# Products that nobody reads, added on TensorE at three places of a vision-tower kernel

## The reference

```python
h = tok(x)                                  # patches @ W_lin.T + b, class token, positions
h = h + attn(layernorm(h))                  # 16 query heads of 16, one shared key/value head
h = h + ffn0(layernorm(h))                  # two factored products, gated by entmax15 of 16 logits
h = h + delta(layernorm(h))                 # causal delta rule: solve (I - A0) A = I, read out
h = h + moe(layernorm(h))                   # 8 experts, arg-max router, 256 -> 1024 -> 256, gelu
```

```python
z = z / 2 - max(z / 2);  zs = sort descending(z)
mean, meansq = cumsum(zs) / k, cumsum(zs * zs) / k
tau = mean - sqrt(clip((1 - k * (meansq - mean**2)) / k, 0))
a = square(clip(z - tau[support - 1], 0))       # support = number of tau <= zs
```

## Time and profile before

| | us |
|---|---|
| median of 3 runs | 780.35 (780.12 to 784.51) |
| profiled execution, its own time | 781.44 |
| its span, first to last instruction | 779.7 |
| PE busy | 672.8 (86% of the span) |
| DVE busy | 419.7 (54%) |
| ACT / POOL busy | 246.8 / 292.6 |
| mean granted TensorE clock | 0.925 of full |

### The profile page before, as it was taken

One profiled execution on the slowest core, in us unless ns is written; L12 is line 12 of the kernel. 1 busy time (PEld: TensorE's weight loads), 2 busy tenths in 40 slices (PEclk: granted clock), 3 DMA queues, 4 the chain that ended last, 5 costly groups with the idle time before them and its releaser, 6 DMA issues.

```text
span 779.7 us, 13703 instructions
## 1 busy us (share of the span) xinstructions
PE 672.8 (86%) x4576; PEld 512.7 (66%) x4576; DVE 419.7 (54%) x1120; ACT 246.8 (32%) x679; POOL 292.6 (38%) x483
## 2 busy tenths in 40 slices
PE   5899999999997614999999589495999999999994
PEld 3566776676765413899999567373667676676763
DVE  2456677777665475244389999557233333333331
ACT  0123333333333114344444256261032323222231
POOL 2344544544444100165566777360222222223220
PEclk9899999999998755899999999896799999999998
DMA  8311001111100000000011216698101111211110
GB/s 302 123 36 32 24 21 34 37 36 37 37 2 1 1 0 2 1 6 8 22 24 32 43 45 236 254 362 309 54 28 55 44 59 41 62 41 51 53 34 14
DMA packets 25070, 50.73 MB, mean 65 GB/s; under 512 B 15611, under 2 KB 15741, under 8 KB 24363
## 3 DMA queue, kind: packets, MB, share of 16 engines
q1 hardware_dynamic: 21387, 35.36, 14.1%
q0 software_dynamic: 3328, 10.23, 4.3%
q10 hardware_dynamic: 288, 4.27, 1.3%
HBM read 39.99 MB, written 9.86 MB: 64 GB/s over the span
## 4 chain that ended last, share of the span: by engine, by line
PE 45%; DVE 7%; issue 4%; POOL 3%; ACT 0%; POOLq 0%; DVEq 0%; ACTq 0%
PE psum L1192 12%; PE psum L1168 11%; PE psum L1389 5%; PE psum L1401 4%; PE psum L1181 3%; PE psum L1435 2%; DVE work L1741 1%; PE psum L1369 1%; PE psum L1011 1%; DVE arena_w L1748 1%; PE psum L1379 1%; POOL work L1900 1%; PE psum L1411 1%; PE psum L1441 1%; POOL work L1889 1%
## 5 line engine op out<-in xcount | busy, mean ns | idle before, releaser
L1265 ACT ACTIVATE work<-psum,cst 128x128 f32<-128x128 f32 x208 | 56.6, 383 | 144.1 <-PE psum L1181 144.1
L1168 PE MATMUL psum<-arena_w,work 128*128 x208 | 93.7, 593 | 1.3 <-DVE work L1219 1.3
L1192 PE MATMUL psum<-arena_w,work 128*128 x416 | 94.2, 379 | 0.4 <-ACT work L1265 0.4
L1130 POOL DMA_INDIRECT out<-work,row_i x26 | 25.8, 990 | 158.0 <-DVE work L1241 158.0
L1192 PEld LDWEIGHTS psum<-arena_w,work 128*128 128x128 f32 x416 | 77.1, 190 | 10.5 <-issue 1.1
L1228 DVE COPY work<-psum 128x512 f32<-128x512 f32 x52 | 36.0, 692 | 67.7 <-PE psum L1168 57.4
L347 PE MATMUL psum<-arena_w 128*111 128x256 f32 x264 | 64.3, 397 | 4.9 <-DMA arena_w<-in_pack 4.9
L712 POOL TENSOR_TENSOR arena_w<-arena_w,work 101x592 f32<-101x592 f32 x33 | 39.6, 1200 | 71.8 <-DVE work L578 71.8
L1168 PEld LDWEIGHTS psum<-arena_w,work 128*128 128x128 f32 x208 | 37.5, 190 | 38.8 <-issue 38.8
L347 PEld LDWEIGHTS psum<-arena_w 128*111 128x111 f32 x264 | 46.8, 183 | 19.6 <-issue 9.6
L703 POOL TENSOR_TENSOR arena_w<-arena_w 128x296 f32<-128x296 f32 x66 | 44.0, 690 | 20.7 <-DVE arena_w L546 20.7
(11 more groups left out here) (220 smaller groups left out, 1332.4 us busy)
## 6 DMA issues: line engine op xcount, KB each, us to landing
arena_w<-in_w SPq DMA_DIRECT2D x2, 4096.0 KB, 13.6
arena_w<-in_x SPq DMA_DIRECT2D x22, 333.0 KB, 3.0
x_rows<-tokens SPq DMA_DIRECT2D x22, 192.0 KB, 5.2
arena_w<-in_pack ACTq DMA_DIRECT2D x1, 2442.0 KB, 9.2
cst<-in_packc ACTq DMA_DIRECT2D x1, 1727.0 KB, 13.4
arena_w<-in_pack SPq DMA_DIRECT2D x1, 818.5 KB, 7.0
arena_w<-in_pack SPq DMA_DIRECT2D x2, 384.0 KB, 4.3
arena_w<-n_rows SPq DMA_DIRECT2D x8, 85.6 KB, 2.8
```

What stands on the lines that cost most here:

```text
L1130: pool.indirect_dma_start(out_h, bass.IndirectOffsetOnAxis(ap=row_i[:, 2 * i + j:2 * i + j + 1], axis=0), yo[j], None).then_inc(y_stored[j ...
L1168: mm = nc.tensor.matmul(bank[2 * j + f][:, :], xgt[j][:, k * 128:(k + 1) * 128], arena_w1[:, bass.ds(expert * (2 * FF) + (k * FF + f * 512 ...
L1192: mm = nc.tensor.matmul(bank[7][:, 0:D], ht[j][:, g * 128:(g + 1) * 128], arena_w2[:, bass.ds(expert * (FC * D) + g * D, D)], start=(g == ...
L1265: nc.scalar.activation(ht[j][:, g * 128:(g + 1) * 128], bank[4 + f][:, k * 128:(k + 1) * 128], ACT.Gelu, bias=cst[:, bass.ds(expert * FC + ...
```

## The change

Filling products come in at three places, and nothing is taken out or moved otherwise.

- Stage 2: 23 fillers on PE ahead of the wait for `gates_ready`, into banks 6 and 7 in turn.
- Stage 3: a new helper `fill_start` issues 3 fillers in the turn i = 0, behind `first_products(0)` and ahead of `hidden(0)`.
- Routing: 6 fillers instead of 4 between the counting products and the wait for `lanes_ready`; `keep_busy` takes the banks 3 to 7 in turn, for its index would otherwise leave PSUM. The 3 fillers behind the placing stay.

```diff
             @block.tensor
             def _(pe):
+                for k in range(23):
+                    nc.tensor.matmul(bank[6 + k % 2], ident, cst[:, 0:512], start=True, stop=True)
                 pe.wait_ge(gates_ready, 1)
...
             def keep_busy(pe, times):
 
                 for k in range(times):
-                    nc.tensor.matmul(bank[3 + k], ident, cst[:, 0:512], start=True, stop=True)
+                    nc.tensor.matmul(bank[3 + k % 5], ident, cst[:, 0:512], start=True, stop=True)
+
+            def fill_start(pe, times):
+
+                for k in range(times):
+                    nc.tensor.matmul(bank[6 + k % 2], ident, cst[:, 0:512], start=True, stop=True)
...
-                keep_busy(pe, 4)
+                keep_busy(pe, 6)
                 for t in range(NT):
                     pe.wait_ge(lanes_ready, t // 4 + 1)
...
                 for i in range(-1, PAIRS + 2):
                     second_products(i - 1)
                     first_products(i)
+                    if i == 0:
+                        fill_start(pe, 3)
```

## The result

| | before | after |
|---|---|---|
| median of the runs of one session | 781.82 us (6 runs, 780.12 to 786.28) | 775.30 us (6 runs, 774.55 to 776.52) |
| ratio, 95% interval | | 0.9911 (0.9881 to 0.994) |
| the same once more, in a later session (e8 below) | 780.36 us | 775.14 us, ratio 0.9945 (0.9922 to 0.9967) |
| span of the profiled execution | 779.7 us | 773.1 us |

The change makes the kernel 4 to 7 us faster. 777.4 was predicted, with 773.0 to 781.5 as the range.

The account below looks back on a forecast made before the run. PE was taken to bound the kernel, running at half clock after waits at the start of stage 3 and in the routing. 0 - 1.8 + 2.1 - 3.6 - 0.7 = -4.0 us from 781.44 gave 777.4 us, range 773.0 to 781.5.

Parts of the forecast that it names:

- The 23 fillers: Stage 2, ahead of the gates' transposes: hidden by DVE's work with 0.2 to 1.5 us to spare, cost 0.
- c: Stage 2: delay until the clock rises under the fillers, taken as 3.4 to 6.0 us; they end at 297.4 + c/2.
- Transposes and copies: End of stage 2: the 22 transposes start at full clock and the last copy ends sooner, gain 1.8 us.
- Three fillers: Stage 3, behind `first_products(0)`: cost 2.1 us on the path at full clock, 4.6 us at half clock.
- The cold stretch: Start of stage 3, PE at half clock for 9.3 us: gain 3.6 us, between bounds of 2.5 or so and 4.7.
- the fear of the pause: Barrier between stages 2 and 3, about 302.7 to 304.4: the clock may be lost, leaving 2.5 or so of 4.7 us.
- The routing: Two more fillers let placing start at full clock: gain 1.2 us, 0.5 charged back behind, net 0.7 us.
- Stages behind move as a whole: Behind feed-forward: later engines' chains start from its end, so those stages shift unchanged.
- Rival A: Between stages 2 and 3: clock lost in the pause, three fillers at half clock; gain about 2, 779.4 us; chance 0.20.
- Rival B: Stage 3 and routing: clock holds through the pause and all placing products; -8.7, 772.7 us; chance 0.08.
- Rival C: Stage 2: fillers get the clock late or never and overrun the gates; slower, up to 793.8 us; chance 0.06.
- rival D: Start of stage 3: the 10.17 us cold stretch is only the profiled execution's; 780.0 us; chance 0.20.

Follow-up runs that it names:

- e8: The whole change run once more, in a later session, against the kernel before; 775.14 us, ratio 0.9945.
- e6: The whole change with 32 instead of 23 fillers ahead of the gates; one execution, 784.31 us.
- e1: The kernel before plus only the 23 fillers ahead of the gates' transposes; 774.93 us, ratio 0.9937.
- e4: The whole change without the three fillers of `fill_start`; 774.79 us, ratio 0.9934.
- e10: The whole change with 2 instead of 3 fillers behind the placing; 778.40 us, ratio 0.9965.
- e3: The kernel before with only the routing's fillers raised from 4 to 6; 780.12 us, ratio 1.0003.
- e11: The kernel before, unchanged, profiled a second time; one execution, 778.45 us.
- e2: The kernel before plus only the three fillers behind `first_products(0)`; 779.29 us, ratio 0.9989.
- e5: The whole change with 15 instead of 23 fillers ahead of the gates; one execution, 778.85 us.
- e7: The whole change with one filler added in the pause, one instead of three behind `first_products(0)`, four in the routing; 777.36 us, ratio 0.9969.

## Why the prediction was right

- The 23 fillers. 297.4 + c/2 with c = 5.3 and a start 1.2 us sooner gives 298.9; they ended at 299.2, with 0.19 us to spare where 0.2 to 1.5 were forecast. No cost, and e6 shows what it is when the cover is gone.
- Transposes and copies: -1.8 forecast, -1.80 measured, in the profile and again in e1 and e4 (26.64 and 26.65).
- Three fillers: +2.1 forecast, +1.78 measured. The 0.3 lies within the overlap of neighbouring PE records.
- The cold stretch: -3.6 forecast, -4.62 measured against the profile of before, which is its upper bound of 4.7: the clock held. Taking a value between the two bounds was a hedge, and neither the profile of the changed kernel nor e8 or e10 lies between them. e1, e4 and e6 show that the fear of the pause was right: there the clock is lost for 3.4 us, in e6 under the three fillers themselves. With them or without them the sum is the same within 0.15 us.
- The routing: -0.7 forecast, -1.69 in the profiles. Neither number is shown to be the change's: e3's ratio is 1.0003, and e11 has the short placing without the two fillers. This term of the sum has no support in the runs.
- "Stages behind move as a whole" held within 0.3 us against e11, where the delta rule's second half took 88.30 us at a mean clock of 0.87, as in the changed kernel (88.33, 0.87). The +0.95 us against the first profile (0.89) are that execution's. In other versions the stretch took up to 91.1 us at 0.82, and the forecast allowed nothing for that.
- The time. 777.4 was added up from an execution of 781.44 us, 1.1 us above the median of its runs. Between the two profiled executions the times differ by 6.6 us, where the sum has 4.0. Of the 2.6 us missing, 1.0 is the cold stretch, 0.3 the three fillers and 1.2 the scatter ahead of stage 2. The delta rule and the routing together are -0.74 us in the profiles beside the forecast's -0.7; as neither part is shown to be the change's, that agreement is luck.

Rival A did not come about in the three profiles of the whole change's first stages. Its loss of the clock behind the pause is seen in e1 and e4, which have no three fillers, and in e6, where they took 4.43 us. Its page, the Trainium skill's "TensorE: Matmul & The Clock Gate", section "Part 4: PE-mode transpose", says that transpose mode does not count as PE being busy in the usual way. The runs are divided: in the first profile of before the clock rose at the end of the 22 transposes, and in e3 3.1 us after they began; in e11 and e2 it did not rise under them, and in the changed kernel it held through them. Rival B's full size did not come: placing stayed at half clock for 5.84 us. Rival C needs a clock that comes later than 6.4 us; in the nine profiles with fillers ahead of the gates it came 5.3 to 6.1 us after they began. Of rival D, 1.2 us hold against e11 and 0.25 against e3.

The three terms of stages 2 and 3 add up to -1.8 + 1.8 - 4.6 = -4.6 us against the first profile of before. Against e11 they are -1.9 + 0.2 - 1.7 = -3.4 us, for there the first groups of stage 3 were at half clock too. The second session's ratio of 0.9945 is 4.3 us. The first session's 0.9911 is 7.0 us (4.7 to 9.3), and what is above 4.6 in it goes with the runs of before: their median was 781.82 us there, with 784.51 and 786.28 among six, and 780.46, 780.36 and 779.81 in the later sessions (52 runs), while the changed kernel had 775.30 and 775.14. The medians of the second session are 5.2 us apart; up to 1 us of that is put down to no part.

## What to carry to other kernels

Where TensorE waits long for another engine and is the bound right behind the wait, fill the wait with products that nobody reads, up to just before the awaited result: what they buy is the clock at the first real product and in the turns behind it. Fillers that end 7 us early lose most of it (e5), and each one too many costs its full 0.83 us (e6). Ahead of short waits on the path fillers trade about one for one (e1 against the whole change), unless dense work follows for which the clock would be lost (e10: 0.1 to 0.2 us for 2.6, in the profiled execution). A version that gains a us upstream has to be timed as a whole, since the later losses of the clock may eat it (e7). And one profile of before is one sample: its routing and its delta rule each differed by 1 to 2 us from those of a second profile of the same kernel (e11).

## What was not expected of the hardware

- The same instructions of the delta rule's second half took 87.4 to 91.1 us, with the mean granted clock between 0.89 and 0.82. The kernel before alone gave 87.38 and 88.30; what decides it, no run isolates.
- Placing products (52 moving columns behind 128 weight columns) never raised the clock in up to 9.6 us of nearly uninterrupted work, and where it was full at their start it fell 0.7 to 2.1 us later. Whether they lost it or the pause of 1.6 to 4.0 us ahead of them did, no run separates.
- Transposes alone raised the clock in one execution of the kernel before, and in e3, and not in e11 and e2.
- In e6 the fillers had run at full clock for 24.9 us (281.5 to 306.4), and 5.8 us after their end the clock was lost all the same, with the transposes, a pause of 1.55 us and the first products of stage 3 between.
